# The first stage of a transformer layer rearranged: loads on two queues, weight folding ahead of the chunk loop, routing in four column tiles, one normalisation moved to POOL

## The chip, the cores and the metric

The kernel runs on one core of a Trainium2 chip. The time is the device time of one execution in microseconds (us), the median of three runs. The engines are TensorE (PE, whose weight loads are shown as PEld), VectorE (DVE), ScalarE (ACT), GpSimd (POOL) and SyncE (SP). Each executes its own queue in order, and they meet only at semaphores. DMAs are issued by SP, ACT and POOL and run on 16 shared DMA engines.

## The reference, cut to what matters

Input is a float32 tensor of 32 sequences, 256 tokens, 128 features, 8,192 tokens in all.

```python
xn = layernorm(x)                       # no gain, no bias
attn(xn):                               # low-rank attention + MLP block
    x1 = layernorm(xn, ln1_g, ln1_b)    # xn normalised a second time
    Q = einsum('bsd,dhr,hre->bhse', x1, q_U, q_V) + q_b     # K and V alike; 16 heads of 8
    h = xn + softmax(mask(Q K^T / sqrt(8))) V @ out_U @ out_V + out_b
    return h + gelu(layernorm(h, ln2_g, ln2_b) @ fc1_U @ fc1_V + fc1_b) @ fc2_U @ fc2_V + fc2_b
ffn(xn):                                # 9 experts, top 2 of each token
    probs = softmax(xn @ Wr)            # Wr is 128 x 9
    w, idx = top_k(probs, 2); w = w / sum(w)
    return sum over the two of w * (silu(xn @ Wg[e]) * (xn @ Wu[e])) @ Wd[e]
out = x + attn(xn) + ffn(xn)
```

## The kernel before, in words

Tokens are handled as 64 tiles of 128, in 16 chunks of 4 tiles. Four stages run one after another, each a block that all engines leave together: `prepare`, `attention`, `experts`, `mlp_and_combine`. Only `prepare` (L155 to L623) is changed. It has five kinds of work.

**Loads.** SP issues four loads of `x` (L240). ACT issues everything else: three `U` matrices, six pieces of the `V` matrices, 24 small loads (L309 to L325), the router weights (L326), and the expert weights in five DMAs (L327 to L330). Only then does ACT compute.

**Statistics.** DVE takes the statistics of all 64 tiles (L498) and turns them into mean and reciprocal deviations for the first and the second normalisation (L510 to L525).

**Fold.** The low-rank pairs are multiplied out once. PE waits for all small loads (L401) and turns `U` (L407 to L413), ACT copies the result out (L335 to L340), PE multiplies (L421), ACT copies again (L346 to L348). The products for the output projection and the MLP (L463 to L467), the scaling of the folded weights by ACT (L391 to L396) and the seven bias products on PE (L485 to L489) come after the chunk loop, some of them after routing.

**Chunk loop.** For each chunk DVE normalises four tiles into `xn` (L533), ACT scales them by the second reciprocal deviation into `xnr` (L357), PE transposes `xnr` (`turn`, L433), ACT copies the bank to `xt` (L364), and PE multiplies each transposed tile, as weights, with the 9 router columns (`score`, L441). DVE copies the 36 logits and multiplies the factor back (L540). SP stores `xn` and `xt` to DRAM in the order xt(c), xn(c+2) (L244, L248). Tiles `xn`, `xnr` and `xt` have two buffers each. The order of the queues is written out: PE does turn(c+2), score(c+1); ACT does scale, copy; DVE does normalise(c+3), copy_logits(c).

**Routing.** DVE picks the top two experts of every token and computes the slots (L569 to L617), with PE counting in between (L472 to L481). Meanwhile POOL issues 17 DMAs that blank the 8.8 MB table `slot_x` (L290), which begin when all `xn` are normalised. SP leaves the block only when these, and all stores, have landed (L259 to L263).

## Time and profile before

| what | value |
|---|---|
| median of 3 runs (lowest, highest) | 1107.15 us (1103.68, 1111.54) |
| the profiled execution's own time | 1107.88 us |
| its span, first to last instruction | 1106.2 us |
| busy share of PE, DVE, ACT, POOL over the span | 91%, 65%, 51%, 35% |
| mean granted TensorE clock | 0.929 of full speed |
| first stage: `prepare` | 0 to 122.2 us |

The first stage is a ninth of the span. It is read by itself, since the busy shares over the whole span are those of attention and the experts. "Granted clock" 1.00 stands for 2.4 GHz and 0.50 for 1.2 GHz.

### The profile page before, as it was taken

The page shows a single profiled execution, that of the slowest core. Times are in us where ns is not written, and L with a number is a line of the kernel's source. Part 1 is how long each engine was busy: PE and PEld are TensorE (multiplying, and loading weights), DVE is VectorE, ACT ScalarE, POOL GpSimd, SP SyncE. Part 2 cuts the span into 40 slices and gives each one's busy share as a digit, 9 for nine tenths or more (in the row PEclk, how much of TensorE's full clock was granted, in tenths as well). Part 3 has the DMA queues.
Part 4 walks back from the last instruction along what each step waited for, and adds up shares of the span by engine and source line. Part 5 has one row for each costly group of instructions (what it writes and reads, how often), then busy time and mean ns, then how long its engine had stood idle before and what let it go on. Part 6 is the DMA issues. An engine that isn't in the chain of part 4 may idle for free. (4 is left out here: it accounts for less than half of the span.)

```text
span 1106.2 us, 25514 instructions
## 1 busy us (share of the span) xinstructions
PE 1001.9 (91%) x7780; PEld 797.5 (72%) x7812; DVE 716.7 (65%) x3239; ACT 565.2 (51%) x1285; POOL 388.9 (35%) x509
## 2 busy tenths in 40 slices
PE   0797478999999999999999997999999999949997
PEld 0696255666666666666666655999999999939996
DVE  5344566777777777777777773555555554547887
ACT  0372025565566556556656674555555555525442
POOL 1003532434443343444334330444444444420110
PEclk9655659999999999999999997999999999969999
DMA  8669542444444444444444301222222222155774
GB/s 223 192 228 360 135 79 69 116 107 104 105 109 112 108 116 107 104 104 108 111 110 107 93 29 46 62 61 66 68 62 68 65 62 59 54 167 166 233 235 125
DMA packets 146754, 128.17 MB, mean 116 GB/s; under 512 B 18560, under 2 KB 128512, under 8 KB 146624
## 3 DMA queue, kind: packets, MB, share of 16 engines
q1 hardware_dynamic: 117344, 72.45, 23.8%
q0 software_dynamic: 17808, 47.35, 15.9%
q10 hardware_dynamic: 11472, 6.75, 2.3%
q8 instruction: 68, 1.11, 0.4%
q14 instruction: 62, 0.51, 0.2%
HBM read 57.68 MB, written 43.13 MB: 91 GB/s over the span
## 5 line engine op out<-in xcount | busy, mean ns | idle before, releaser
L1201 DVE CUSTOM_DVE_ANT_0 att_masked_st<-att_m_ps,att_mask_st 128x128 bf16<-128x128 f32 (+1 forms) x1024 | 312.0, 353 | 108.7 <-PE att_m_ps L916 72.1
L1106 ACT ACTIVATE att_probs<-att_t_ps 128x512 f32<-128x512 f32 x384 | 229.4, 598 | 190.5 <-PE att_t_ps L940 140.8
L834 POOL DMA_INDIRECT slot_x<-att_xs,att_slot_now x128 | 128.6, 1004 | 265.6 <-PE att_t_ps L940 169.1
L1369 POOL DMA_INDIRECT y_scratch<-moe_y,moe_row_now x136 | 131.3, 966 | 154.1 <-issue 68.7
L1509 DVE TENSOR_TENSOR moe_hidden<-moe_gate,moe_up_ps 128x352 f32<-128x352 f32 x136 | 70.9, 521 | 114.5 <-issue 84.2
L1429 PE MATMUL moe_y_ps<-w_down,moe_hidden_t 128*128 (+1 forms) x816 | 114.0, 276 | 2.4 <-issue 1.8
L1469 ACT ACTIVATE moe_gate<-moe_gate_ps 128x352 f32<-128x352 f32 x136 | 63.1, 464 | 95.9 <-PE moe_up_ps L1412 95.9
L940 PE MATMUL att_t_ps<-att_mask_ts,att_ident_b 128*128 128x256 bf16 (+1 forms) x352 | 111.1, 316 | 0.0
L1429 PEld LDWEIGHTS moe_y_ps<-w_down,moe_hidden_t 128*128 128x128 f32 (+1 forms) x816 | 101.7, 191 | 3.9 <-issue 3.8
L1201 DVE DVE_READ_ACCUMULATOR2_ANT att_row_max<- 128x1 f32 x1024 | 84.9, 83 | 0.2
L939 PE MATMUL att_t_ps<-even_stack,att_k_stack 97*128 97x512 f32 x192 | 81.2, 423 | 4.2 <-DMA even_stack<-att_neg_max 4.1
L955 PE MATMUL att_pv_ps<-att_probs,att_v_ones 128*32 128x256 f32 x1024 | 81.8, 391 | 0.0
L939 PE MATMUL att_t_ps<-att_odd_stack,att_k_stack 97*128 97x512 f32 x192 | 80.5, 420 | 1.3 <-DMA att_odd_stack<-att_neg_max 0.9
L940 PEld LDWEIGHTS att_t_ps<-att_mask_ts,att_ident_b 128*128 128x128 bf16 x384 | 37.5, 98 | 61.1 <-issue 54.7
L916 PE MATMUL att_m_ps<-att_k_stack,even_stack 96*128 96x256 f32 x256 | 71.2, 364 | 10.8 <-DMA even_stack<-att_q_lo 8.7
L1662 PEld LDWEIGHTS mlp_o_ps<-w,mlp_mid 128*128 128x128 f32 x512 | 66.4, 191 | 5.2
L916 PE MATMUL att_m_ps<-att_k_stack,att_odd_stack 96*128 96x256 f32 x256 | 68.1, 348 | 0.2 <-DVE att_row_max L1201 0.2
L1421 PE MATMUL moe_hidden_ps<-ident,moe_hidden 128*128 128x128 f32 (+1 forms) x408 | 67.1, 273 | 0.1
L1662 PE MATMUL mlp_o_ps<-w,mlp_mid 128*128 128x128 f32 x512 | 66.9, 275 | 0.0
L1702 ACT ACTIVATE mlp_mid<-mlp_f_ps,mlp_bias 128x512 f32<-128x512 f32 x64 | 44.0, 687 | 44.5 <-PE mlp_f_ps L1654 43.1
L916 PEld LDWEIGHTS att_m_ps<-att_k_stack,even_stack 96*128 96x128 f32 x256 | 42.8, 205 | 32.8 <-issue 28.4
L829 POOL DMA_DIRECT2D att_k_stack<-att_k_hi x64 | 36.8, 575 | 57.1 <-PE att_t_ps L940 30.7
(247 smaller groups left out, 2134.3 us busy)
## 6 DMA issues: line engine op xcount, KB each, us to landing
slot_x<-prep_blank POOLq DMA_DIRECT2D x17, 516.0 KB, 12.8
moe_x<-slot_x SPq DMA_DIRECT2D x34, 258.0 KB
att_xs<-xn_scratch SPq DMA_DIRECT2D x32, 256.0 KB
att_k_stack<-att_k_hi POOLq DMA_DIRECT2D x64, 128.0 KB
mlp_rows<-y_scratch POOLq DMA_DIRECT2D x16, 512.0 KB, 5.0
xn_scratch<-prep_xn SPq DMA_DIRECT2D x16, 256.0 KB, 2.6
xt_scratch<-prep_xt SPq DMA_DIRECT2D x16, 256.0 KB, 2.1
att_xt<-xt_scratch SPq DMA_DIRECT2D x16, 256.0 KB, 2.9
```

What stands on the lines that cost most here:

```text
L834: pool.indirect_dma_start(env["slot_x"][:], bass.IndirectOffsetOnAxis(ap=slot_now[c.parity][:, col:col + 1], axis=0), xs[c.parity][:, t, k ...
L916: last = pe.matmul(ps[:, n * SEQ:(n + 1) * SEQ], q[0:ROWS, g, i, hi:hi + P], k[0:ROWS, g, lo:lo + SEQ], start=True, stop=True)
L939: pe.matmul(by_lane, keys, q[rows, g, lanes, queries], start=True, stop=False, skip_group_check=True)
L940: pe.matmul(by_lane[:, :, 0:P], ident_b[:], mask_ts[:, lanes, :], start=False, stop=True, skip_group_check=True).then_inc(scores_done, 1)
L955: last = pe.matmul(pv_ps[32 * i:32 * i + 32, g * SEQ:(g + 1) * SEQ], v_ones[c.parity][:, 2 * b, g * LANES + i, :], pt, start=(g % 2 == 0), ...
L1106: act.activation(probs[:, m % PT, :], t_ps[m % 2][:], ACT.Exp).then_inc(exp_done, 1)
L1201: last = dve.tensor_tensor_reduce(out=masked_st[m % 2][:, part], in0=m_ps[m % 2][:, part], in1=mask_st[:, SEQ - width:], scale=1.0, scalar ...
L1369: pool.indirect_dma_start(env["y_dram"][:], bass.IndirectOffsetOnAxis(ap=row_now[q.parity][:, t:t + 1], axis=0), y[c.parity][:], None).the ...
L1421: last = pe.transpose(hidden_ps[0:n, k * P:(k + 1) * P], hidden[c.parity][:, col:col + n], ident[:])
L1429: last = pe.matmul(y_ps[:, 0:P], hidden_t[c.parity][0:n, k * P:(k + 1) * P], down_cols[0:n, ds(e * (NCH * P) + k * P, P)], start=(k == 0), ...
L1509: dve.tensor_tensor(hidden[c.parity][:], gate[c.parity][:], up_ps[c.parity][:, 0:FF], ALU.mult).then_inc(hidden_done, 1)
L1662: last = pe.matmul(o_ps[c.parity][:, t * P:(t + 1) * P], mid[c.parity][:, k, t * P:(t + 1) * P], w2[:, k, :], start=(k == 0), stop=(k == H ...
```

## The change

ACT keeps nine loads (`U`, `V`, counted on a semaphore of their own) and the router load. The 24 small loads and then the expert weights go to SP, behind the loads of `x` and before the first store. PE's fold of q, k, v waits for the nine loads only; the rest of the fold, with the scaling and the bias products, is done in front of the chunk loop. POOL makes `xnr` straight from `x` with the product of both reciprocal deviations; ACT's `scale` is gone. `score` has the router weights (padded from 9 to 32 columns with zeros) as the stationary side and the transposed tile as the moving side, each of the four tiles on its own 32 columns of the array. Its result is turned by 90 degrees, so ACT copies it to `by_expert`, and PE transposes that back (`score_back`), from where DVE reads the logits. DVE's `normalise` no longer waits for `xnr`. Loops that indexed with `ds` are written out.

```diff
-w_router = s.sb("w_router", [P, EXPERTS])
+w_router = s.sb("w_router", [P, 32])
...
+both_rstd = s.sb("both_rstd", [P, tiles])
+by_expert = s.two("by_expert", [P, P])
...
+        small = [0]
+        def load(dst, src, columns=False):
+            sp.dma_start(dst, src, allow_slow_non_contiguous=columns).then_inc(small_loaded, 16)
+            small[0] += 16
+        load(out_u[:], w["out_U"])
+        load(out_v[:], w["out_V"])
+        load(fc1_u[:], w["fc1_U"])
+        load(fc1_v[:], w["fc1_V"])
+        load(fc2_u[:], w["fc2_U"].rearrange("(c p) r -> p c r", p=P))
+        load(fc2_v[:], w["fc2_V"])
+        for dst, name in ((ln1_g, "ln1_g"), (ln1_b, "ln1_b"), (ln2_g, "ln2_g"), (ln2_b, "ln2_b")):
+            load(dst[:], w[name].rearrange("(p o) -> p o", o=1), True)
+        load(v_b[:], w["v_b"].rearrange("h e -> (h e)").partition_broadcast(P))
+        load(out_bias[:], w["out_b"].partition_broadcast(P))
+        load(fc2_bias[:], w["fc2_b"].partition_broadcast(P))
+        load(fc1_b[:], w["fc1_b"].rearrange("(c p) -> p c", p=P), True)
+        for dst, name in ((q_b, "q_b"), (k_b, "k_b")):
+            by_lane = w[name].rearrange("(g i) (e o) -> i e g o", i=LANES, o=1)
+            for i in range(LANES):
+                load(dst[32 * i:32 * i + 32, :], by_lane[i], True)
+        assert small[0] == 16 * N_SMALL
+        sp.wait_ge(x_loaded[XL - 1], 16)
+        sp.dma_start(w_gate_up[:, :, 0:FF].bitcast(F32), w["Wg"].rearrange("e d i -> d e i")).then_inc(experts_loaded, 16)
+        sp.dma_start(w_gate_up[:, :, FF:2 * FF].bitcast(F32), w["Wu"].rearrange("e d i -> d e i")).then_inc(experts_loaded, 16)
+        for c, (at_row, rows) in enumerate(FF_CHUNKS):
+            sp.dma_start(w_down[0:rows, :, c, :], w["Wd"][:, at_row:at_row + rows, :].rearrange("e p d -> p e d")).then_inc(experts_loaded, 16)
         def store_xn(c):
+            sp.wait_ge(xn_ready, c + 1)
+            sp.dma_start(env["xn_tiles"][:, c * TPC:(c + 1) * TPC, :], xn[c % 2][:]).then_inc(xn_stored[c % 2], 16)
...
+        store_xn(0)
+        store_xn(1)
+        for c in range(chunks):
+            store_xt(c)
+            if c + 2 < chunks:
+                store_xn(c + 2)
...
+        pool.memset(w_router[:], 0.0).then_inc(router_cleared, 1)
...
+        pool.wait_ge(ln_ready, 1)
+        for c in range(chunks):
+            if c >= 2:
+                pool.wait_ge(xt_turned, c - 1)
+            for t in range(TPC):
+                tile = c * TPC + t
+                last = pool.tensor_scalar(xnr[c % 2][:, t, :], x_all[:, tile, :], mean[:, tile:tile + 1], both_rstd[:, tile:tile + 1],
+                                          ALU.subtract, ALU.mult)
+            last.then_inc(xnr_ready, 1)
         pool.wait_ge(xn_ready, chunks)
...
+            act.dma_start(u_in[k][:], w[f"{n}_U"].rearrange("d h r -> d (h r)")).then_inc(qkv_loaded, 16)
...
+        act.wait_ge(router_cleared, 1)
+        act.dma_start(w_router[:, 0:EXPERTS], w["Wr"]).then_inc(router_loaded, 16)
...
         act.wait_ge(fold_pe, 7)
         for k in range(2):
             act.copy(raw_qkv[:, k, :].rearrange("p (i e g) -> p g i e", i=LANES, e=DH),
                      bank[6][:, k * P:(k + 1) * P].rearrange("p (g i e) -> p g i e", i=LANES, e=DH)).then_inc(fold_act, 1)
         act.copy(raw_qkv[:, 2, :], bank[6][:, 2 * P:3 * P]).then_inc(fold_act, 1)
+        act.wait_ge(fold_pe, 8)
+        act.copy(ut_small[0:RANK_OUT, 0:P], bank[7][0:RANK_OUT, 0:P]).then_inc(fold_act, 1)
+        act.copy(ut_small[0:RANK_MLP, P:2 * P], bank[7][0:RANK_MLP, P:2 * P]).then_inc(fold_act, 1)
+        act.wait_ge(fold_pe, 9)
+        act.copy(ut_fc2[:], bank[0][0:RANK_MLP, :]).then_inc(fold_act, 1)
+        act.wait_ge(small_loaded, 16 * N_SMALL)
         act.mul(g_q[:], ln1_g[:], float(DH) ** -0.5).then_inc(fold_act, 1)
...
+        def copy_xt(c):
+            act.wait_ge(xt_turned, c + 1)
+            if c >= 2:
+                act.wait_ge(xt_stored[c % 2], 16 * (c // 2))
+            act.copy(xt[c % 2][:], bank[c % 2][:]).then_inc(xt_ready, 1)
+        def copy_by_expert(c):
+            act.wait_ge(routed_t, c + 1)
+            if c >= 2:
+                act.wait_ge(logits_ready, c - 1)
+            act.copy(by_expert[c % 2][:], bank[2 + c % 2][:, 0:P]).then_inc(by_expert_ready, 1)
+        copy_xt(0)
+        for c in range(chunks):
+            if c + 1 < chunks:
+                copy_xt(c + 1)
+            copy_by_expert(c)
+        act.wait_ge(gap_ready, 1)
+        act.activation(gap_exp[:], gap[:], ACT.Exp).then_inc(gap_exped, 1)
...
     @block.tensor
     def _(pe):
         pe.wait_ge(const_ready, N_CONST)
+        pe.wait_ge(qkv_loaded, 16 * N_QKV)
         for r in range(6):
             for j in range(4):
                 pair = 4 * (r % 2) + j
                 last = pe.transpose(bank[r][0:PR, j * P:(j + 1) * P], u_in[r // 2][:, pair * PR:(pair + 1) * PR], ident[:])
             last.then_inc(fold_pe, 1)
...
+        pe.wait_ge(small_loaded, 16 * N_SMALL)
+        pe.transpose(bank[7][0:RANK_OUT, 0:P], out_u[:], ident[:])
+        pe.transpose(bank[7][0:RANK_MLP, P:2 * P], fc1_u[:], ident[:]).then_inc(fold_pe, 1)
+        for c in range(HCH):
+            last = pe.transpose(bank[0][0:RANK_MLP, c * P:(c + 1) * P], fc2_u[:, c, :], ident[:])
+        last.then_inc(fold_pe, 1)
+        pe.wait_ge(fold_act, 12)
+        pe.matmul(bank[1][:, 0:P], ut_small[0:RANK_OUT, 0:P], out_v[:], start=True, stop=True)
+        pe.matmul(bank[2][:], ut_small[0:RANK_MLP, P:2 * P], fc1_v[:], start=True, stop=True)
         for c in range(HCH):
             last = pe.matmul(bank[3][:, c * P:(c + 1) * P], ut_fc2[:, c * P:(c + 1) * P], fc2_v[:], start=True, stop=True)
         last.then_inc(fold_pe, 1)
+        pe.wait_ge(fold_act, 21)
+        pe.matmul(bank[6][:, 0:1], raw_qkv[:, 0, :], ln1_b[:], start=True, stop=True)
+        pe.matmul(bank[6][:, 1:2], raw_qkv[:, 1, :], ln1_b[:], start=True, stop=True)
+        for c in range(HCH):
+            pe.matmul(bank[6][:, 2 + c:3 + c], raw_w1[:, c * P:(c + 1) * P], ln2_b[:], start=True, stop=True)
+        pe.matmul(bank[6][:, P:2 * P], b_rows[:], raw_qkv[:, 2, :], start=True, stop=True).then_inc(fold_pe, 1)
+        def turn(c):
+            pe.wait_ge(xnr_ready, c + 1)
+            if c >= 2:
+                pe.wait_ge(xt_ready, c - 1)
+            for t in range(TPC):
+                last = pe.transpose(bank[c % 2][:, t * P:(t + 1) * P], xnr[c % 2][:, t, :], ident[:])
+            last.then_inc(xt_turned, 1)
+        def score(c):
+            pe.wait_ge(xt_ready, c + 1)
+            if c >= 2:
+                pe.wait_ge(by_expert_ready, c - 1)
+            for t in range(TPC):
+                last = pe.matmul(bank[2 + c % 2][32 * t:32 * t + 32, 0:P], w_router[:], xt[c % 2][:, t * P:(t + 1) * P], start=True, stop=True,
+                                 skip_group_check=True)
+            last.then_inc(routed_t, 1)
+        def score_back(c):
+            pe.wait_ge(by_expert_ready, c + 1)
+            if c >= 2:
+                pe.wait_ge(logits_copied, c - 1)
+            pe.transpose(bank[4 + c % 2][:, 0:P], by_expert[c % 2][:], ident[:]).then_inc(logits_ready, 1)
+        pe.wait_ge(router_loaded, 16)
+        turn(0)
+        turn(1)
+        score(0)
+        for c in range(chunks):
+            if c + 2 < chunks:
+                turn(c + 2)
+            if c + 1 < chunks:
+                score(c + 1)
+            score_back(c)
         pe.wait_ge(gap_ready, 1)
+        pe.wait_ge(logits_copied, chunks)
...
+        step(dve.tensor_tensor(both_rstd[:], rstd[:], rstd2[:], ALU.mult))
+        dve.sem_inc(ln_ready, 1)
         step(dve.tensor_tensor(std2[:], var[:], rstd2[:], ALU.mult))
...
+        def normalise(c):
+            if c >= 2:
+                dve.wait_ge(xn_stored[c % 2], 16 * (c // 2))
...
+        def copy_logits(c):
+            dve.wait_ge(logits_ready, c + 1)
+            dve.tensor_tensor(logits[:, c * TPC:(c + 1) * TPC, :], bank[4 + c % 2][:, 0:P].rearrange("p (t e) -> p t e", e=32)[:, :, 0:EXPERTS],
+                              std2[:, c * TPC:(c + 1) * TPC].unsqueeze(2).to_broadcast([P, TPC, EXPERTS]), ALU.mult).then_inc(logits_copied, 1)
+        normalise(0)
+        normalise(1)
+        normalise(2)
+        for c in range(chunks):
+            if c + 3 < chunks:
+                normalise(c + 3)
+            copy_logits(c)
...
-        dve.wait_ge(fold_pe, 13)
+        dve.wait_ge(fold_pe, 11)
...
```

## Rows read from the trace of the kernel before

**Rows 1.** Busy time by windows: PE, PEld, DVE, ACT, POOL, clock, DMA share, GB/s.
```profile
70.00:80.00 10.00, 10.00 (x50) 10.00 (x51) 5.06 (x22) 7.23 (x21) 0.00 (x0) 0.50 0.65 215
300.00:310.00 10.00, 9.93 (x91) 6.22 (x92) 7.85 (x46) 6.55 (x12) 1.94 (x2) 1.00 0.45 136
```

**Rows 2.** Timeline of the loads (start, duration, both in us); last line: landing of `v_v`.
```profile
8.53 2.73 ACTq L298 DMA_DIRECT2D prep_ln_g<-in_L_attn_ln_g  x1
10.84 2.92 SPq L240 DMA_DIRECT2D prep_x_all<-in_L_attn_hidden_states  x1
24.34 0.53 ACTq L298 DMA_DIRECT2D prep_fc_v<-in_L_attn_fc_V  x1
26.75 10.77 ACTq L330 DMA_DIRECT2D w_down<-in_L_ffn_Wd  x3
...
DMA to landing us min/median/max: 7.0/7.3/7.6
```

**Rows 3.** Timeline of the fold before the chunk loop.
```profile
27.70 1.92 PE L407 MATMUL prep_bank<-ident,prep_u_q 128*96 128x128 f32 x8 [27.70 <-DMA prep_fc_v<-in_L_attn_fc_V]
32.30 0.23 DVE L525 TENSOR_TENSOR prep_std<-prep_var,prep_rstd 128x64 f32<-128x64 f32 x1
40.12 3.54 PEld L421 LDWEIGHTS prep_bank<-prep_v_q,prep_ut 96*128 96x128 f32 x16
50.69 0.61 ACT L346 COPY prep_raw_qkv<-prep_bank 128x128 f32<-128x128 f32 x2 [8.05 <-PE prep_bank L421]
52.81 2.19 PE L433 MATMUL prep_bank<-ident,prep_xnr 128*128 128x128 f32 x8 [2.21 <-ACT prep_xnr L357]
```

**Rows 4.** Timeline of one period of the chunk loop.
```profile
80.92 0.90 PEld L433 LDWEIGHTS prep_bank<-ident,prep_xnr 128*128 128x128 f32 x4
81.81 1.83 PEld L441 LDWEIGHTS prep_bank<-prep_w_router,prep_xt 128*128 128x128 f32 x8
82.26 0.59 ACT L364 COPY prep_xt<-prep_bank 128x512 f32<-128x512 f32 x1 [0.69 <-PE prep_bank L433]
83.37 0.90 PEld L433 LDWEIGHTS prep_bank<-ident,prep_xnr 128*128 128x128 f32 x4
```

**Rows 5.** Timeline of a store of `xn` and the normalisation that waits for it.
```profile
60.15 0.36 SPq L244 DMA_DIRECT2D xn_scratch<-prep_xn  x1
62.45 1.12 DVE L533 TENSOR_SCALAR prep_xn<-prep_x_all,prep_mean,prep_rstd 128x128 f32<-128x128 f32 x4 [0.80 <-DMA xn_scratch<-prep_xn]
```

**Rows 6.** Timeline after the loop: rest of the fold, end of routing.
```profile
93.15 0.50 PEld L463 LDWEIGHTS prep_bank<-prep_out_v,prep_ut_small 96*128 96x128 f32 x2 [0.45 <-issue]
97.69 0.59 ACT L385 COPY w<-prep_bank 128x512 f32<-128x512 f32 x1 [1.12 <-PE prep_bank L467]
102.98 0.39 ACT L391 ACTIVATE wq<-prep_raw_qkv,prep_g_q 128x128 f32<-128x128 f32 x1
111.22 0.59 PE L485 MATMUL prep_bank<-prep_ln_b,prep_raw_qkv 128*128 128x1 f32 x2
113.81 0.78 PE L489 MATMUL prep_bank<-prep_raw_qkv,prep_b_rows 128*128 128x128 f32 x2
122.23 3.51 POOL L811 MEMSET even_stack<- 128x4096 f32 x1 [27.48 <-POOLq L234]
```

**Rows 7.** Timeline in attention: matmuls of 32 columns, and the next 128-column one.
```profile
305.91 0.64 PE L961 MATMUL att_pv_ps<-att_probs,att_v_ones 128*32 128x128 f32 x16
306.49 0.51 PE L916 MATMUL att_m_ps<-att_k_stack,att_odd_stack 96*128 96x256 f32 x2
```

**Rows 8.** Groups by line, POOL's operations: busy us, mean ns, idle before.
```profile
L850 POOL TENSOR_TENSOR att_xn<-att_xn,out_bias 128x512 f32<-128x512 f32 x16 | 20.7, 1291 | 0.3
L274 POOL TENSOR_SCALAR_AFFINE_SELECT ident<-ident 128x128 f32<-128x128 f32 x1 | 0.3, 290 | 0.2 <-POOL prep_ones L271 0.2
```

**Rows 9.** The blanking of `slot_x`: POOL's issues, then the window in which DMA falls silent.
```profile
85.62 8.08 POOL L290 DMA_DIRECT2D slot_x<-prep_blank  x15 [80.99 <-DVE prep_xn L533]
112.00:116.00 4.00, 2.58 (x12) 2.28 (x11) 3.63 (x15) 0.00 (x0) 0.00 (x0) 0.50 0.07 28
```

More of the change, by code:

```diff
@@ L388, in _ @@
-                act.activation(gap_exp[:], gap[:], ACT.Exp).then_inc(gap_exped, 1)
                 act.wait_ge(fold_act, 16)
@@ L423, in _ @@
                 last.then_inc(fold_pe, 1)
-                pe.wait_ge(fold_act, 9)
-                pe.wait_ge(router_loaded, 16)
-                def turn(c, first):
-                    pe.wait_ge(xnr_ready, c.index + 1)
-                    if not first:
-                        pe.wait_ge(xt_ready, c.index - 1)
-                    for t in range(TPC):
-                        last = pe.transpose(bank[c.parity][:, t * P:(t + 1) * P], xnr[c.parity][:, t, :], ident[:])
-                    last.then_inc(xt_turned, 1)
@@ L436, in score @@
-                def score(c, of_four, first):
-                    pe.wait_ge(xt_ready, c.index + 1)
-                    if not first:
-                        pe.wait_ge(logits_copied, c.index - 3)
-                    for t in range(TPC):
-                        last = pe.matmul(bank[2 + of_four][:, t * EXPERTS:(t + 1) * EXPERTS], xt[c.parity][:, t * P:(t + 1) * P],
-                                         w_router[:], start=True, stop=True)
-                    last.then_inc(logits_ready, 1)
@@ L465, in _ @@
-                pe.wait_ge(fold_act, 9)
+                pe.wait_ge(small_loaded, 16 * N_SMALL)
[5 more added lines that the diff above has]
+                pe.wait_ge(fold_act, 12)
```

154 lines of the change are left out of this document (15 added, 139 removed).

## The prediction, made before the changed kernel was run

> **What bounds the kernel now.** The change touches the first stage alone, so I read the chain of waits only to see that everything runs in sequence behind that stage (the chain that ended last begins in the MLP stage and says nothing of `prepare`), and then windows and timeline of `prepare` by itself. Attention's first instruction comes at 122.2 us [rows 6], so a microsecond taken from the stage is one from the total as long as nothing else holds the stage's end. The stage has three stretches.
>
> First, up to 52.8 us: PE starts its first transpose at 27.70 us, released by the last small load, and the chunk loop's first transpose at 52.81 us [rows 3]. DVE was through with the statistics at 32.5 us [rows 3]; the fold is what is late. It is late because ACT issues loads until 26.75 + 10.77 = 37.5 us [rows 2] before it copies anything, and because 48 small matmuls take from 40.12 to 50.69 us [rows 3].
>
> Second, the chunk loop from 52.8 to 93.15 us, 40.3 us [rows 3, 6]. One period is 83.37 - 80.92 = 2.45 us, and PE fills it: 0.89 us of transposes, then 1.56 us of routing matmuls [rows 4]. In that stretch PE is 10.00 us busy in 10, ACT 7.23, DVE 5.06, DMA 0.65, at a granted clock of 0.50 [rows 1], that is 1.2 GHz.
>
> Third, routing from 93.15 to 122.2 us, 29.1 us [rows 6], mostly a DVE chain with PE counting in between.
>
> **The change part by part.** *Loads and first half of the fold.* ACT now issues only nine loads before the router's. The last of the nine is out before 8.53 us, where ACT now goes on to the small loads, and lands at most 7.6 us later [rows 2]: 16.1 us instead of 27.7 for PE's start. The 24 transposes cost 0.222 us each at the loop's pace (0.89 / 4 [rows 4]), 5.3 us, to 21.4 us; ACT, idle by then, copies beside them. The 48 matmuls cost the same 10.6 us [rows 3], to 32.0 us. I cost them at the slow level of the clock, since nothing denser than before runs there.
>
> *Small loads on SP.* SP is through with issuing `x` at 10.84 + 2.92 = 13.8 us; the 24 small loads took ACT from 8.53 to 24.87 us, 16.3 us, and the last landed 27.70 - 24.34 = 3.4 us after issue [rows 2, 3]. So they are in at 13.8 + 16.3 + 3.4 = 33.5 us at the latest; about 31 us if the 2.73 us of the first [rows 2] is a full queue that SP does not meet. The fold goes on at about 33.0 us (ends 32.0 and 33.5).
>
> *Second half of the fold, now ahead of the loop.* Six transposes at 0.222 and a copy, 2.0 us, to 35.0; products and their copies as at 93.15 to 97.69 + 0.59, 5.1 us, to 40.1; five scalings at 0.39, 1.9 us, to 42.0; bias products 111.22 to 113.81 + 0.78, 3.4 us [rows 6], to 45.4 us. Where they come from they were hidden: the products under DVE's routing, the bias products under the same chain, so their removal there gains nothing. Here they are on the path, 12.4 us of it, and are the price of starting the loop with PE and ACT clear. The loop starts at 45.4 us instead of 52.8: **7.4 us gained** (bounds of the start 43 and 49).
>
> *Expert weights on SP.* They follow the small loads, from 30.1 us, for 10.8 us for three [rows 2] and about 1.2 for two short ones: SP reaches its first store at 42 us, which lands some 3 us later. Behind that store stand DVE's third normalisation and, behind that, the first copy of logits, which is due at 45.4 + 3.5. Cost nothing; a further 4 us in that queue would show one for one.
>
> *POOL's normalisation.* No POOL operation of this kind is in the trace. From below: one pass over 128x128 takes 0.29 us; a two-input pass over 128x512 takes 1.29, a quarter of it 0.32 [rows 8]. From above: subtract and multiply as two passes, 0.58. I take 0.35, near the quarter since it has the same width and one read less, against two scalars per partition to fetch: 1.4 us for a chunk (1.2 to 2.3). The first two chunks are ready before 37 us, since its inputs are there at 32.5. The extra DVE multiplication costs 0.23 us [rows 3], off the path.
>
> *Column tiles.* Attention's 16 matmuls of 32 columns with 128 moving columns take 0.64 us, and the next full-width one starts 0.58 us after the first of them [rows 7], at a granted clock of 1.00 [rows 1]. At half of that, the eight of a chunk take 0.6 us instead of 1.56. The upper end is no overlap at all, 1.6. The new transpose back is 0.22, its copy on ACT at most 0.59 where 1.27 of scaling disappear [rows 4]. PE: 0.89 + 0.6 + 0.22 = 1.7 us for a chunk.
>
> The trace shows full-width and 32-column matmuls following each other without a visible gap [rows 7]. The Trainium skill (TensorEngine Tiling (Array Packing), Tiling Modes) says that changing the tiling mode drains the engine, and the loop changes it twice per chunk; by that PE's 1.7 us would be longer by two drains, still below what comes next.
>
> *What bounds the loop next.* DVE may write a buffer of `xn` only when its store has landed: 1.12 us of normalising, 2.30 us from issue to the normalisation that waited for it [rows 5], and 0.1 to 0.9 us until SP comes to it behind a store of `xt`. That makes 3.5 to 4.3 us for two chunks, 1.8 to 2.15 for one. I take a period of 2.1 us. Around 14 full periods stand about 5.0 us: two turns, a copy and the first scores 2.4, and at the end a score, a copy, a transpose back and a copy of logits 2.6. The loop takes 5.0 + 14 x 2.1 = 34.4 us against 40.3: **5.9 us gained**.
>
> *End of the stage.* Routing is unchanged, 29.1 us. The stage ends at 45.4 + 34.4 + 29.1 = 108.9 us. The blanking DMAs begin 7.5 us ahead of the loop's end and were silent by about 112 us [rows 9], some 27 us after their start: 72.3 + 27 = 99 us, still covered by routing. If the loop's last part were much faster they would come next, with 10 us to spare.
>
> Sum: 7.4 + 5.9 = 13.3 us. The profiled execution took 1107.9 us, so 1094.6; it lies 0.7 us above the median of the runs shown. I forecast **1094.5 us**.
>
> **The rivals.** *(A) DVE and POOL exclude each other.* The trace cannot tell: POOL does no arithmetic in the loop today. If every normalising instruction of either engine held the other up, a chunk would cost 1.12 + 1.4 = 2.5 us, and the stage's gain would be 7.4 + 40.3 - 5.0 - 35.0 = 7.7 us: 1100 us. Against it: DVE's time for four is partly start-up of each instruction, in which POOL could get through. By this kernel's rows the engines are 1.1 and 1.4 us busy, so even in turns they barely exceed the old period. The Trainium skill (SBUF — State Buffer, Who interferes with whom) states such an exclusive port pair for DVE's `tensor_scalar` in a two-port mode against any GpSimd operation; no row here bears it out or refutes it.
>
> *(B) POOL is slow, and the kernel slower than before.* The place is POOL's four instructions per chunk. At 0.58 us each and in turns with DVE the period is 4 x 0.58 + 1.12 = 3.4 us, the loop 52.6 us, the total 1107.9 - 7.4 + 12.3 = 1112.8 us. It decides from a period of (40.3 + 7.4 - 5.0) / 14 = 3.05 us, which is 0.48 us per POOL instruction in turns with DVE, or 0.76 alone.
>
> *(C) Column tiles do not overlap here*, with four tiles of different data: PE 0.89 + 1.6 + 0.22 and the switches, 2.8 us; gain 3.5 us, 1104.4 us. Against it stands attention's row.
>
> *(D) The loop starts late.* Small loads behind `x` in SP's queue, or the stores behind 4.5 MB of expert weights, cost 5 us more: 1099.5 us.
>
> *(E) PE is granted the full clock* somewhere in the fold, now that it runs in one piece. It halves at most the 27 us of fold: up to 10 us more, some 1088 us. Against it: PE was just as busy between 40 and 50.7 us and in the loop, and stayed at 0.50 [rows 1].
>
> **How the numbers follow.** Forecast 0.47, A 0.21, B 0.09, C 0.07, D 0.09, E 0.07. The forecast's own range, start 43 to 48 and period 1.8 to 2.3, is 1088 to 1100. A measurement can tell about 1% (11 us) from no change; that needs a period below 2.3 at the forecast's start. Faster by more: 0.9 of the forecast, E, and a third of A and D, 0.59. Slower by more than 1%: B beyond 3.8 us per period or several delays at once, 0.05. Within: 0.36. The range runs from 1087 (E, and the fast end of the forecast) to 1106 (A, C, D with the scatter of the runs); B and the far end of E are left out.
>
> **What would show it.** Right: PE's first transpose near 16 us; q, k, v products done near 32; the first `xnr` transposes at 45 us and 2.1 us apart; DVE idle before `xn` on the store; router matmuls of a chunk in about 0.6 us; POOL 0.35 us each; POOL's blanking from 72 us; attention from 109 us. Wrong: POOL's instructions above 0.48 us, or PE waiting for `xnr` each chunk (A, B); router matmuls 0.2 us apart (C); a wait of DVE or PE for loads beyond 46 us (D). The forecast would also fail if attention, started 13 us earlier, gave part of it back in its own first chunks.

## The result, and the profile after: 1112.05 us instead of 1094.5

Over 20 runs each the changed kernel took 1112.05 us (1109.84 to 1114.47), the kernel before 1107.58 us (1102.48 to 1111.54): a ratio of 1.0037, interval 1.0026 to 1.0048. That is within 1%, on the slow side, and 17.5 us above the forecast. A second series of the same kernel gave 1110.78 against 1107.50 us, 1.0038 (1.0024 to 1.0053). The profiled execution took 1112.97 us, of which the span is 1111.2.

I read the changed kernel in the same order as the old one. First the timeline of PE from the first transpose to the chunk loop (start and duration in us; what stands in brackets is idle time and who ended it):

```profile
13.87 1.92 PE L404 MATMUL prep_bank<-ident,prep_u_q 128*96 128x128 f32 x8 [13.87 <-DMA prep_v_v<-in_L_attn_v_V]
17.80 1.86 PE L411 MATMUL prep_bank<-prep_v_q,prep_ut 96*128 96x16 f32 x16
21.30 1.94 PE L411 MATMUL prep_bank<-prep_v_v,prep_ut 96*128 96x16 f32 x16
30.05 0.45 PE L416 MATMUL prep_bank<-ident,prep_out_u 128*96 128x128 f32 x1 [6.81 <-DMA prep_k_b<-in_L_attn_k_b]
43.15 1.92 PE L440 MATMUL prep_bank<-ident,prep_xnr 128*128 128x128 f32 x8
```

The fold starts at 13.87 us instead of 27.70 [rows 3], runs to 23.24 us, then PE stands for 6.81 us until the last small load is in, and the loop's first transpose comes at 43.15 us. Before, it came at 52.81 us [rows 3]: 9.7 us gained, 2.3 more than forecast. Now windows of that stretch, of the loop and of the same 10 us as in [rows 1] (PE, PEld, DVE, ACT, POOL busy; clock; DMA share; GB/s):

```profile
16.00:24.00 8.00, 7.23 (x63) 7.11 (x61) 7.76 (x39) 3.16 (x8) 0.00 (x0) 0.96 0.49 141
24.00:31.00 7.00, 0.95 (x5) 0.81 (x6) 6.04 (x29) 0.26 (x2) 0.00 (x0) 0.50 0.28 43
70.00:80.00 10.00, 6.37 (x40) 3.35 (x40) 4.11 (x17) 2.56 (x6) 10.00 (x14) 0.50 0.50 171
```

Two things are new. First, PE ran at the full clock in the middle of the fold: the 48 products take 5.4 us (17.80 to 23.24), where they took 10.6 us [rows 3]. The clock column alone does not show this. It reads 1.00 in the kernel before too, from 28 to 36 us, while eight transposes took 1.92 us there [rows 3], and it reads 1.00 here at 13.87 us, where eight take the same 1.92 us as at 43.15 us and a reading of 0.50. The durations are to be read beside it. Second, in the loop PE fell from 10.00 busy in 10 to 6.37, while POOL went from 0.00 to 10.00: the bound has moved to POOL. One period of the loop shows how, against [rows 4]:

```profile
69.34 8.15 POOL L326 TENSOR_SCALAR prep_xnr<-prep_x_all,prep_mean,prep_both_rstd 128x128 f32<-128x128 f32 x10
73.49 1.11 PE L440 MATMUL prep_bank<-ident,prep_xnr 128*128 128x128 f32 x4 [1.12 <-POOL prep_xnr L326]
74.54 0.66 PE L449 MATMUL prep_bank<-prep_xt,prep_w_router 128*32 128x128 f32 x8
74.64 0.59 ACT L379 COPY prep_xt<-prep_bank 128x512 f32<-128x512 f32 x1 [2.35 <-PE prep_bank L440]
75.12 0.48 PE L457 MATMUL prep_bank<-ident,prep_by_expert 128*128 128x128 f32 x1
75.64 0.20 DVE L535 TENSOR_TENSOR prep_logits<-prep_bank,prep_std 128x36 f32<-128x36 f32 x1 [1.96 <-PE prep_bank L457]
75.75 1.16 DVE L528 TENSOR_SCALAR prep_xn<-prep_x_all,prep_mean,prep_rstd 128x128 f32<-128x128 f32 x4
76.72 0.69 PE L440 MATMUL prep_bank<-ident,prep_xnr 128*128 128x128 f32 x2 [1.12 <-POOL prep_xnr L326]
```

The transposes of two chunks begin 76.72 - 73.49 = 3.23 us apart, where it was 2.45. Everyone else waits: PE for POOL, ACT for PE, DVE for PE. POOL alone has no gap between its instructions. The groups by line give its price (count, busy us, mean ns, idle before):

```profile
L326 POOL TENSOR_SCALAR prep_xnr<-prep_x_all,prep_mean,prep_both_rstd 128x128 f32<-128x128 f32 x64 | 51.6, 818 | 33.2 <-DVEq L520 26.7 <-PE prep_bank L440 6.5
```

The waits of the loop, 43 to 97 us, say who stood for whom (total, times, longest, in us). PE stood 16.5 us for POOL:

```profile
PE prep_bank L440 <- POOL prep_xnr L326: 16.5, 14, 1.8
DVE prep_xn L528 <- DMA xn_scratch<-prep_xn: 15.8, 3, 14.3
ACT prep_xt L379 <- DMA xt_scratch<-prep_xt: 6.3, 2, 3.7
```

POOL itself stood once, for 6.5 us up to 44.2 us: it had filled both buffers of `xnr`, and PE had not begun to empty them. At 0.81 us from start to start (3.23 / 4) its 64 instructions from 31.41 us on would have ended near 83 us without that wait, by estimate, instead of at 89.48.

Last, the timeline at the loop's end and at the stage's end, against [rows 6]:

```profile
89.48 9.19 POOL L332 DMA_DIRECT2D slot_x<-prep_blank  x17
...
93.18 0.20 DVE L535 TENSOR_TENSOR prep_logits<-prep_bank,prep_std 128x36 f32<-128x36 f32 x1 [0.26 <-PE prep_bank L457]
...
122.58 3.51 POOL L802 MEMSET even_stack<- 128x4096 f32 x1 [23.91 <-POOLq L237]
```

The account of the stage: the loop starts 9.7 us earlier, it lasts 93.38 - 43.15 = 50.2 us instead of 40.3, 9.9 us more, and routing takes 29.2 us as before. The stage ends at 122.58 us, where it ended at 122.23. The whole rearrangement is paid back inside the loop.

### The profile page after: what moved, and what is told of

Same layout as the page of the kernel before. It is cut to its first block and busy times, and to the rows that moved or that the text cites. A ratio compares the mean times of both kernels' runs of the same rounds, so it can differ in the third digit from the quotient of the medians.

```text
span 1111.2 us, 25566 instructions
## 1 busy us (share of the span) xinstructions
PE 990.7 (89%) x7796; PEld 770.2 (69%) x7828; DVE 717.9 (65%) x3240; ACT 551.3 (50%) x1237; POOL 440.3 (40%) x574
## 3 DMA queue, kind: packets, MB, share of 16 engines
q8 instruction: 69, 1.13, 0.4%
HBM read 57.68 MB, written 43.13 MB: 91 GB/s over the span
## 5 line engine op out<-in xcount | busy, mean ns | idle before, releaser
L326 POOL TENSOR_SCALAR prep_xnr<-prep_x_all,prep_mean,prep_both_rstd 128x128 f32<-128x128 f32 x64 | 51.6, 818 | 33.2 <-DVEq L520 26.7
## 6 DMA issues: line engine op xcount, KB each, us to landing
slot_x<-prep_blank POOLq DMA_DIRECT2D x17, 516.0 KB, 11.1
```

## The experiments

The theory to be tested: POOL's instruction with two values per partition costs 0.80 us and alone sets the period; the loads, the fold and the column tiles are worth about what was forecast. Rivals: DVE and POOL hold each other up at a shared port; column tiles save nothing; the stores hold the loop; the rearranged stage slows the later stages. "Before" always means the kernel before, run on the same chip beside the experiment; different experiments ran on different chips, so their ratios compare better than their times. The edits are given in short. The end of the stage is read from the same instruction as above, the first one of attention on POOL.

**One edit to the changed kernel: ACT makes `xnr` again.**

```diff
-pool: xnr[c % 2][:, t, :] = (x_all[:, tile, :] - mean) * both_rstd
+act.activation(xnr[c % 2][:, t, :], xn[c % 2][:, t, :], ACT.Identity, scale=rstd2[:, ...])   # after xn_ready, ahead of copy_xt
+dve: normalise(c) waits for xnr_ready again
```

> The changed kernel, but the twice normalised x is made by ACT from xn, as in the kernel before (DVE waits for it again). Theory P (POOL's instructions of 0.8 us are the loop's period and nothing else is): period 2.1 to 2.3 us instead of 3.23, the loop 34 to 37 us instead of 50, the first stage ends near 108 us instead of 122.6. Theory S (the period is held by the stores or by the new chain of copies on ACT as well): period 2.8 us or more, stage end 116 us or later. Theory R for the total (the rest of the kernel, from the stage's end on, is 988.7 us after and 984.0 us before, and the rearranged stage itself costs the rest 4 to 5 us): total = stage end + 989, so 1097 us under P. If the 4.7 us belong to when attention starts or to chance of one profile: stage end + 984, so 1092 us.

Measured: 1101.16 us, ratio 0.9942 (0.9921 to 0.9962); stage end 112.61 us. Taking POOL out of the loop gives back 10 us of the stage. From the third chunk (50.18 us) to the last (80.06 us) PE's transposes are 2.30 us apart in the mean, the upper end of theory P; the stage still ends 4.6 us later than theory P had it. The timeline (SP's issues, DVE, PE) shows what is late next:

```profile
40.86 2.48 SPq L278 DMA_DIRECT2D xn_scratch<-prep_xn  x2
42.42 1.91 PE L443 MATMUL prep_bank<-ident,prep_xnr 128*128 128x128 f32 x8
47.70 2.13 DVE L532 TENSOR_SCALAR prep_xn<-prep_x_all,prep_mean,prep_rstd 128x128 f32<-128x128 f32 x8 [14.48 <-DMA xn_scratch<-prep_xn]
50.18 1.12 PE L443 MATMUL prep_bank<-ident,prep_xnr 128*128 128x128 f32 x4 [5.26 <-ACT prep_xnr L383]
```

The first store of `xn` is issued at 40.86 us, behind the expert weights in SP's queue, and lands near 47.7. DVE has waited 14.48 us for it, ACT scales what DVE made, and PE stops for 5.26 us at the third chunk. This is rival D of the prediction, a late start of the stores. In the changed kernel it is hidden, since POOL makes `xnr` from `x` and is slower anyway.

**One edit to the kernel before: POOL makes `xnr`.**

```diff
-scale(c) on ACT, and DVE's wait for xnr_ready
+POOL's loop over tensor_scalar(xnr, x_all, mean, both_rstd, subtract, mult), as in the changed kernel
```

> The kernel before with only this part of the change: POOL makes xnr, ACT's scale is gone. Loads, fold and router matmuls as before. Theory P: period 3.2 us instead of 2.45, loop longer by about 14 x 0.8 = 11 us, the total 1118 us. Theory X (POOL is slow only beside DVE, or only in the new kernel): period below 2.7 us, total within 4 us of before. The loop starts as before near 52 us.

Measured: 1117.44 us, ratio 1.0087 (1.0060 to 1.0114); stage end 130.64 us, 8.4 us later than before. PE's weight loads show the period, against [rows 4]; the group shows POOL's price in this kernel:

```profile
61.70 0.72 PEld L431 LDWEIGHTS prep_bank<-ident,prep_xnr 128*128 128x128 f32 x4 [0.78 <-POOL prep_xnr L294]
64.90 0.72 PEld L431 LDWEIGHTS prep_bank<-ident,prep_xnr 128*128 128x128 f32 x4 [0.68 <-POOL prep_xnr L294]
```

```profile
L294 POOL TENSOR_SCALAR prep_xnr<-prep_x_all,prep_mean,prep_both_rstd 128x128 f32<-128x128 f32 x64 | 51.1, 813 | 41.1 <-DVEq L524 26.7 <-PE prep_bank L431 14.4
```

The period is 3.2 us (64.90 - 61.70), though loads, fold and router matmuls are as before. This one part of the change costs 8.4 us of the stage and 10.7 us of the median.

**Loads and fold alone**: the changed kernel with ACT's scaling and the old routing.

```diff
+scale(c) on ACT; score(c) with xt as weights and 9 moving columns
-POOL's xnr, w_router of 32 columns, by_expert, score_back
```

> The changed kernel's loads and fold ahead of the loop, with the loop of before (ACT makes xnr, router matmuls 128x128 by 9 columns, no transpose back). If loads and fold are a gain of their own: the loop starts at 43 to 44 us instead of 52.8, its period is 2.45 us as before, the stage ends near 113 us, total 1098 us (or 1103 if the rest loses 5 us). If moving the fold ahead costs what it saves: stage end 120 us or more.

Measured: 1103.70 us, ratio 0.9966 (0.9946 to 0.9986); loop start 42.41, period 2.45 us, stage end 115.81 us.

```profile
69.60 0.90 PEld L441 LDWEIGHTS prep_bank<-ident,prep_xnr 128*128 128x128 f32 x4
72.06 0.90 PEld L441 LDWEIGHTS prep_bank<-ident,prep_xnr 128*128 128x128 f32 x4
```

The loop starts 10.4 us earlier but the stage ends only 6.4 us earlier; the stop on the first store takes the rest. Beside the first experiment, which differs by the column tiles and the transpose back alone, they are worth 115.81 - 112.61 = 3.2 us of the stage.

**POOL's forms measured by themselves**, in its idle time at the start of the changed kernel, on tiles that nothing else uses:

```diff
+for _ in range(2): pool.tensor_copy(out(), trial_in[:, 0:P])
+for _ in range(2): pool.tensor_scalar(out(), trial_in[:, 0:P], 2.0, None, ALU.mult)
+for _ in range(2): pool.tensor_scalar(out(), trial_in[:, 0:P], 1.0, 2.0, ALU.subtract, ALU.mult)
+for _ in range(2): pool.tensor_scalar(out(), trial_in[:, 0:P], at_one[:, 0:1], None, ALU.mult)
+for _ in range(2): pool.tensor_scalar(out(), trial_in[:, 0:P], at_one[:, 0:1], at_one[:, 1:2], ALU.subtract, ALU.mult)
+pool.tensor_scalar(out(4), trial_in[:], at_one[:, 0:1], at_one[:, 1:2], ALU.subtract, ALU.mult)
+for _ in range(2): pool.tensor_tensor(out(), trial_in[:, 0:P], ones[:], ALU.mult)
```

> The changed kernel with 13 more POOL instructions on scratch tiles in POOL's idle time between 5 and 31 us; nothing reads them. 128x128 float32: copy, one operation with a constant, two operations with constants, one operation with a per-partition scalar, two operations with two per-partition scalars, a two-input multiply; and 128x512 with two per-partition scalars. Theory A (the per-partition scalars cost, each a fixed amount): copy and constants near 0.3 us, one scalar 0.5 to 0.55, two scalars 0.8, and 128x512 with two scalars 0.8 + 0.4 to 0.8. Theory B (two operations cost per element): two constants 0.5 to 0.8 us as well, and 128x512 about 2.5 us or more. Theory C (the sharing of ports with DVE costs): two scalars well below 0.8 us here, where DVE takes statistics or idles.

Measured, in the order of the diff (start, duration of the group; x2 is two instructions):

```profile
5.26 0.52 POOL L330 COPY prep_trial<-prep_trial_in 128x128 f32<-128x128 f32 x2
5.77 1.06 POOL L332 TENSOR_SCALAR prep_trial<-prep_trial_in 128x128 f32<-128x128 f32 x2
6.81 1.26 POOL L334 TENSOR_SCALAR prep_trial<-prep_trial_in 128x128 f32<-128x128 f32 x2
8.07 1.18 POOL L336 TENSOR_SCALAR prep_trial<-prep_trial_in,prep_at_one 128x128 f32<-128x128 f32 x2
9.24 1.56 POOL L338 TENSOR_SCALAR prep_trial<-prep_trial_in,prep_at_one 128x128 f32<-128x128 f32 x2
10.80 2.06 POOL L340 TENSOR_SCALAR prep_trial<-prep_trial_in,prep_at_one 128x512 f32<-128x512 f32 x1
12.84 0.44 POOL L342 TENSOR_TENSOR prep_trial<-prep_trial_in,prep_ones 128x128 f32<-128x128 f32 x1
```

A copy costs 0.29 us, as the select of [rows 8] did. One operation with a constant costs about 0.53, with a value per partition 0.59; two operations 0.64 with constants and 0.78 with values per partition. A two-input pass of the same size costs 0.44. So the price hangs on the form, and the two rows that I had taken as nearest are of the cheap forms. Neither theory fits whole: A had the constants near 0.3 us, B had the wide tile at 2.5 us or more, and it took 2.06. The 0.78 is there with POOL by itself, so DVE beside it can account for at most the 0.02 to 0.04 us by which the loop's instruction is longer. This is one execution of one kernel.

**Expert weights issued by POOL instead of SP**, on the first experiment's kernel.

```diff
-sp.dma_start(w_gate_up ..., w_down ...)      # five, ahead of the first store
+pool.dma_start(w_gate_up ..., w_down ...)    # after x_loaded
```

> The kernel of e1 (ACT makes xnr), with the five expert-weight DMAs issued by POOL, which has nothing to do there, and not by SP in front of the first stores. Theory Q (the queue: in e1 the first store of xn goes out at 40.9 us because SP issues weights until then; DVE waits 14.5 us for it and PE 5.3 us behind that): first store near 33 us, no wait of PE at the third chunk, stage end 5 us earlier than e1's 112.6, total 4 to 5 us below e1. Rival (the DMA engines are full with the weights whichever queue issues them, so the store lands as late): the third chunk's wait stays above 3 us, total within 1.5 us of e1.

Measured: 1107.49 us, ratio 1.0012 (0.9998 to 1.0027); stage end 121.12 us. SP's queue was free, and the stage ended 8.5 us later than with the weights on it. PE's timeline, and the DMA share of two windows (second-last number):

```profile
42.61 0.45 PE L419 MATMUL prep_bank<-ident,prep_out_u 128*96 128x128 f32 x1 [16.81 <-DMA prep_k_b<-in_L_attn_k_b]
```

```profile
20.00:30.00 10.00, 5.80 (x37) 5.69 (x36) 8.94 (x42) 0.72 (x3) 4.18 (x5) 0.60 0.87 260
30.00:40.00 10.00, 0.00 (x0) 0.00 (x0) 3.48 (x14) 0.00 (x0) 0.00 (x0) 0.50 1.03 263
```

The weights' transfers fill the 16 engines from 20 us on, and the small loads, issued at the same time, land 12.6 us later than in the changed kernel (42.6 against 30.05 us). The loop starts at 55.71 us instead of 42.42, and with so late a start the third chunk waits only 0.41 us. Neither expectation was met. The queue was part of what makes the first store late: it is issued at 32.80 us instead of 40.86. But the DMA engines are full, and a store takes up to 9.9 us to land where the longest took 6.8. The Trainium skill (DMA: Bandwidth & Descriptors, Issuing engines are not separate DMA queues) says that DMAs of all issuing engines interleave on the same 16 engines; the trace agrees, with the 12.6 us.

**The same, with a wait for the needed loads only.** PE and ACT wait for the first ten small loads (the weights and gains that the fold uses); the other fourteen have a semaphore of their own.

```diff
-pe.wait_ge(small_loaded, 16 * N_SMALL)     # ACT alike
+pe.wait_ge(fold_loaded, 16 * N_FOLD)       # the first ten; dve waits for the rest before q_bias
```

> The kernel of e5, and PE's second half of the fold waits for the first ten small loads only (matrices and layer norm gains), not for all 24; the others are waited for by DVE at the end. In the changed kernel PE stands still from 23.2 to 30.05 us for the last of them. If that wait is the start's limit: the loop starts 5 to 7 us earlier than in e5 (near 37 us), but not before the statistics allow, total 4 to 6 us below e5, near 1091 us. If DVE's statistics and first normalisation (33 us) and the stores set the pace instead: less than 2 us below e5.

Measured: 1095.12 us, ratio 0.9911 (0.9886 to 0.9936); loop start 39.03, stage end 109.86 us. PE's wait is gone: the turn of `out_U` starts at 25.95 us. The loop starts 16.7 us and the stage ends 11.3 us earlier than in the kernel above; I had expected 5 to 7 us. The third chunk still stops (PE, DVE, PE):

```profile
25.95 0.43 PE L422 MATMUL prep_bank<-ident,prep_out_u 128*96 128x128 f32 x1
44.12 2.14 DVE L535 TENSOR_SCALAR prep_xn<-prep_x_all,prep_mean,prep_rstd 128x128 f32<-128x128 f32 x8 [10.16 <-DMA xn_scratch<-prep_xn]
46.60 1.11 PE L446 MATMUL prep_bank<-ident,prep_xnr 128*128 128x128 f32 x4 [5.07 <-ACT prep_xnr L386]
```

The first store of `xn` goes out at 32.97 us, 7.9 us earlier than behind the weights in SP's queue (40.86), and has landed at 44.12, only 3.6 us earlier (47.70): it is 11.1 us on its way instead of 6.8.

**The same, with ACT making `xnr` straight from `x`**, so that it hangs on no store.

```diff
-act.wait_ge(xn_ready, c + 1)
-act.activation(xnr, xn,    Identity, scale=rstd2)
+act.activation(xnr, x_all, Identity, scale=both_rstd, bias=both_shift)   # both_shift = -mean * both_rstd
```

> The kernel with split small loads (its PE and ScalarE wait only for the first ten small loads, ScalarE scales xn), with one edit: ScalarE makes xnr straight from x, with scale = product of the reciprocal deviations and bias = -mean times it, so PE's transposes no longer hang on DVE's xn and its stores. Theory S (the stop of 5.07 us at the third chunk is the store of xn landing late and holding DVE, then ScalarE): the stop vanishes, the period becomes that of ScalarE, 1.27 + 0.59 + 0.27 = 2.1 us, the stage ends near 104 us instead of 109.9, total about 1090 against 1095.1. Rival T (the store of xt waits in the same queue behind the store of the third xn, so ScalarE's copy of the fourth chunk stops instead): PE stops at the third or fourth chunk for about 5 us as before, stage end 108 to 110, total 1094 to 1095.

Measured: 1091.53 us, ratio 0.9852 (0.9829 to 0.9874); stage end 105.17 us. The stop has shrunk from 5.07 to 0.78 us, and ACT sets the period (2.18 us), as PE's and ACT's timelines show:

```profile
43.13 1.12 PE L448 MATMUL prep_bank<-ident,prep_xnr 128*128 128x128 f32 x4 [0.78 <-ACT prep_xnr L387]
...
66.70 1.66 ACT L387 ACTIVATE prep_xnr<-prep_x_all,prep_both_shift,prep_both_rstd 128x128 f32<-128x128 f32 x4
68.25 0.58 ACT L373 COPY prep_xt<-prep_bank 128x512 f32<-128x512 f32 x1
68.72 0.27 ACT L379 COPY prep_by_expert<-prep_bank 128x128 f32<-128x128 f32 x1
68.88 1.67 ACT L387 ACTIVATE prep_xnr<-prep_x_all,prep_both_shift,prep_both_rstd 128x128 f32<-128x128 f32 x4
```

The theory of the store holds, its rival (the store of `xt` in the same queue stops the fourth chunk instead) does not. This is the fastest kernel of the study.

**Column tiles undone in that kernel.**

```diff
-score(c) in four column tiles, copy_by_expert(c), score_back(c)
+pe.matmul(bank[2 + c % 4][:, t * EXPERTS:(t + 1) * EXPERTS], xt[..t..], w_router[:])
```

> The same kernel as the one in which ScalarE makes xnr straight from x, with one part of the change undone: routing has the transposed tiles as weights and nine moving columns again, four weight loads a chunk, and there is no transpose back and no copy of by_expert. Theory O (column tiles overlap, 0.58 to 0.66 us for a chunk against 1.56): PE is 0.89 + 1.56 = 2.45 us a chunk and sets the period at 2.45 instead of ScalarE's 2.1; with the shorter end of the loop the kernel is 3 to 5 us slower than the one with column tiles. Rival C (the column tiles save nothing once the transpose back and its copy are counted): the same time or faster.

Measured: 1094.92 us, ratio 0.9896 (0.9874 to 0.9917); stage end 107.86 us, PE's period 2.46 us:

```profile
54.48 1.09 PE L441 MATMUL prep_bank<-ident,prep_xnr 128*128 128x128 f32 x4
56.94 1.09 PE L441 MATMUL prep_bank<-ident,prep_xnr 128*128 128x128 f32 x4
```

The column tiles are worth 2.7 us of the stage and 3.4 us of the median here, with 3.2 us in the pair above. Rival C is refuted.

**Only POOL's price changed**, in the changed kernel: a plain copy, and one operation with one value per partition. The first leaves out the normalisation in `xnr`, the second the mean, so neither kernel computes the layer; all other instructions are the changed kernel's.

```diff
-pool.tensor_scalar(xnr, x_all, mean, both_rstd, ALU.subtract, ALU.mult)
+pool.tensor_copy(xnr, x_all)                              # first kernel
+pool.tensor_scalar(xnr, x_all, both_rstd, None, ALU.mult) # second kernel
```

> The changed kernel with one edit: POOL copies x into xnr (a plain copy of 128x128, 0.29 us in the run of POOL's forms) instead of subtracting and multiplying by two values per partition; xnr is then x without its normalisation. Theory P (the price of POOL's instruction, 0.80 us, is the failed step, the others held but for the late first store): period about 2.2 us, a stop of some 5 us of the third chunk on the first store of xn, stage end 112 to 113, total 1100 to 1102. Rival F (the forecast's other steps hold in full, no stop): stage end 108, total 1096 to 1097. Rival X (the loop is held by something else than POOL, as the store of xn or PE): period above 2.6, total above 1104.

> The changed kernel with one edit: POOL multiplies x by one value per partition (0.594 us in the run of POOL's forms, near the upper bound of 0.58 of the forecast) and does not subtract the mean; xnr is then x without its mean taken off. Theory P: four instructions set the period, 4 x 0.594 + 0.03 = 2.41 us, with the stop on the first store partly hidden: stage end 113 to 116, total 1102 to 1105, so that the forecast's upper bound would still have been faster than before. Rival X: the period stays above 2.8 us and the total above 1107.

Measured: with the copy 1096.84 us, ratio 0.9920 (0.9890 to 0.9950), stage end 107.59 us; with one operation 1098.61 us, 0.9940 (0.9918 to 0.9961), stage end 109.73 us. The groups of POOL in the two kernels, and PE's transposes of the second:

```profile
L326 POOL COPY prep_xnr<-prep_x_all 128x128 f32<-128x128 f32 x64 | 16.3, 299 | 51.3 <-DVEq L519 27.0 <-PE prep_bank L439 24.2
```

```profile
L326 POOL TENSOR_SCALAR prep_xnr<-prep_x_all,prep_both_rstd 128x128 f32<-128x128 f32 x64 | 37.5, 604 | 34.5 <-DVEq L519 26.4 <-PE prep_bank L439 8.1
```

```profile
72.11 1.12 PE L439 MATMUL prep_bank<-ident,prep_xnr 128*128 128x128 f32 x4 [0.20 <-POOL prep_xnr L326]
74.42 1.11 PE L439 MATMUL prep_bank<-ident,prep_xnr 128*128 128x128 f32 x4 [0.20 <-POOL prep_xnr L326]
```

From 0.80 us to 0.60 and 0.30 the stage ends 12.9 and 15.0 us earlier, and no other line was touched. (The granted clock moved with it: 0.63 and 0.75 from 60 to 80 us, against 0.50 in the changed kernel.) At 0.60 the period is 2.31 us and POOL still sets it. At 0.30 POOL waits for PE, and the loop takes 35.2 us (43.16 to 78.38), where the forecast had 34.4. Its period is 2.17 us in the mean, where the forecast had 2.1, and now the stores weigh as the forecast said: ACT waits 20.3 us (14 times) for stores of `xt`, DVE 22.8 us (12 times) for stores of `xn`. I had expected a stop of 5 us on the first store in these two; the longest stop of PE was 2.9 us in the first, and both came in 3 to 6 us below my figures, in the first near those of rival F.

**The later stages.** The changed kernel and the kernel before were run again as they are, twice, the second time the changed one in five rounds.

> The kernel before once more, for a second profile of it. The rest of the kernel, from the stage's end to the end of the span, took 984.0 us in its profile and 985.5 to 989.2 us in the profiles of five kernels whose stages after the first are the same code. If that is chance of one profile (theory N), this one gives 985 to 989, and its first stage may end away from 122.2 us with the clock's phase, by up to 5 us. If the rearranged first stage makes the rest slower (theory R), it gives 983 to 985 again, with the stage's end at 122.

> The changed kernel once more, for a second profile of it. Under theory N the rest of the kernel takes 985 to 989 us and need not repeat its 988.7; under theory R it takes 988 to 990 again. The first stage ends within 1 us of 122.6, since POOL sets its loop and POOL's time does not hang on TensorE's clock.

> The changed kernel as it is, against the kernel before, to see whether what its medians have beyond the first stage (about 4 us, where the ends of the first stage differ by 0.5 us) is there again. Theory R (the changed stage makes the later stages slower by 3 to 4 us): ratio 1.003 to 1.005 again. Rival N (chance of that set of runs): ratio 0.999 to 1.002.

> The kernel before as it is, for one more profile of the stages behind the first: between the end of the first stage and the end, 984 us as in its two other profiles (theory R) or anywhere between 982 and 989 us as in the other kernels (rival N).

Measured, from the end of the first stage to the end of the span: before 984.0, 983.8 and 989.7 us; changed 988.6, 984.1 and 986.6 us. The profiles overlap, and the one of `before_b` lies above all of the changed kernel. But the ratio of the five rounds was 1.0038 again, so the difference of the medians, 3.3 to 4.5 us, is not chance. The three profiles of each kernel show less of it: their spans are 1.4 us apart in the mean (1107.5 and 1108.9). Of this 0.75 us are there at the end of the first stage (121.68 and 122.43) and all 1.4 us at the first product with V in attention (162.9 and 164.3). The other 2 to 3 us of the medians are in no profile.

The other runs have the same gap. If the median is compared with that of the kernel before beside it, and the movement of the stage's end (from 121.68) is taken off, 2.5 to 5.0 us are left in the six series of kernels in which SP issues the expert weights, and 0.5 to 2.0 us in the five others. With POOL's copies the stage ends 14.1 us earlier and the median falls by 9.1 us only. Each figure rests on one profile for the stage's end, and no run was made for the split, so it is a hint; where the time goes is left open.

## Why the prediction was wrong, point by point

- *POOL's normalisation*: this is the step that failed. I priced the instruction at 0.35 us with an upper bound of 0.58; it measured 0.78 alone and 0.80 to 0.82 in the loop. The lower value was a quarter of a two-input pass over 128x512, 0.32; the same pass over 128x128 takes 0.44. The bound was two plain passes of 0.29 each; yet a pass that takes even one value per partition costs 0.59. The bound was no bound, because it was built from rows of another form of instruction.
- *What bounds the loop next*: I said the store of `xn`, at 2.1 us. It was POOL, at 3.23 us. Over 14 periods that is 14 x 1.13 = 15.8 us, and it explains the miss of the stage: 108.9 + 15.8 - 2.3 (earlier start) = 122.4 us, against 122.58 measured. With POOL's price put near the forecast's, the mean period falls to 2.17 and 2.34 us, the stage ends at 107.6 and 109.7 us (forecast 108.9) and the total is 1096.8 and 1098.6 us. For the stage the other steps of the forecast held together, with errors that cancel in part: a start 2.3 us early against a loop 0.8 us long.
- *A microsecond of the stage is one of the total*: this I took without a price, and it held only in part. With POOL's copies the stage ended 1.3 us before the forecast and the total lay 2.3 us above it; the 2.5 to 5.0 us that such kernels lose against their stage are not explained.
- *Rival B* is what happened, by its second reading: it put the point of decision at 0.76 us per instruction with POOL alone. With the start as measured the point is (40.3 + 9.7 - 5.0) / 14 = 3.21 us for a chunk, 0.80 for an instruction, and there the stage came out level; the rest of the slowdown is not in the stage. That its figure of 1112.8 us lies near the 1112.05 measured is luck: it stands for 0.58 us in turns with DVE and a later start. I gave it 0.09, and left it out of the range.
- *Rival A*, DVE and POOL excluding each other: refuted in this kernel. In full turns a chunk would take 4 x 0.78 + 1.12 = 4.24 us; it took 3.23. POOL's instruction takes 0.80 to 0.82 us in the loop and 0.78 alone; DVE's four take 1.16 us against 1.12 [rows 5]. The Trainium skill (SBUF — State Buffer, Who interferes with whom) says that the shared port pair is an exclusive lock, which DVE's `tensor_scalar` takes when it runs in a two-port mode. The trace shows 0.01 to 0.04 us per instruction; in which mode DVE ran, no run shows.
- *Loads and first half of the fold*: PE started at 13.87 us (forecast 16.1) and was through at 23.24 (forecast 32.0), since it was granted the full clock; *rival E* came true in part. It bought nothing, because the small loads landed at 30 us (forecast 31 to 33.5) and PE stood for them. In the two other profiles of the same kernel the clock fell back sooner, PE was through at 25.97 and 26.28 us, and the loop began at 42.83 and 43.13 us all the same. A forecast with the clock at half speed hid that wait.
- *Second half of the fold*: forecast 12.4 us from the last small load to the loop; measured 43.15 - 30.05 = 13.1. The start was forecast at 45.4, and came at 43.15.
- *Expert weights on SP*: I costed them at nothing, with "a further 4 us would show one for one". In the changed kernel they cost nothing, as POOL hides them; without POOL they cost a stop of about 5 us. The place was right, and the term that was too small is the way of the first store: 6.8 us to land where I had put 3. Taking the weights out of SP's queue brings its issue 7.9 us forward and its landing 3.6 us, since the DMA engines stay full. (The weights are 4,752 KB by their issues; I had written 4.5 MB.)
- *Column tiles*: 0.6 us for a chunk forecast, 0.58 to 0.66 measured, at half clock. Their worth, 2.7 to 3.2 us, only shows when POOL is out of the way. Where PE fills its time, as in the kernel with POOL's copies from 54 to 58 us (window and two transposes below), a chunk costs it 1.85 us, 0.14 more than the forecast's 0.89 + 0.6 + 0.22. Whether that is the price of switching between tiling modes, which the prediction named, the trace does not separate.

```profile
54.00:58.00 4.00, 4.00 (x28) 2.58 (x29) 2.92 (x13) 1.69 (x5) 1.96 (x8) 0.50 0.89 297
54.19 1.06 PE L439 MATMUL prep_bank<-ident,prep_xnr 128*128 128x128 f32 x4
56.04 1.06 PE L439 MATMUL prep_bank<-ident,prep_xnr 128*128 128x128 f32 x4
```

- *End of the stage*: routing 29.2 us as forecast, and the blanking stays hidden though it began only at 89.48 us.

## What to carry to other kernels

Moving work to an idle engine is priced by that engine's row for that very form of instruction: number of operations, and whether its operands are constants, values per partition or tiles. Where no such row exists, the bound from above must not be built from the cheapest form, nor from a share of a wider tile: two passes of the two-input form at its 128x128 price, 0.88 us, would have been a bound here, two copies were not. The break-even price is to be compared with that bound before anything else. When a bound moves, look for the waits that the new bound hides (here the first store, the wait for all small loads); removing them took the ratio from 0.9942 to 0.9852 (1101.16 to 1091.53 us).

## What the runs showed of the hardware that I had not expected

POOL's time per 128x128 float32 instruction runs from 0.29 us (copy) over 0.44 (two tiles), 0.53 (one constant), 0.59 (one value per partition) and 0.64 (two constants) to 0.78 us (two values per partition); the last takes 2.06 us on 128x512, so by estimate from these two sizes some 0.35 us of it do not depend on size.

PE's busy time alone does not tell which clock TensorE is granted. The kernel before had PE 10.00 busy in 10 at 0.50 [rows 1]. The kernel with POOL's copies had PE 4.00 busy in 4 at 0.50 from 54 to 58 us, read 1.00 from 60 us on, and fell back to 0.50 near 67 us, when PE had been busy for 1.3 of 4 us (PE, PEld, DVE, ACT, POOL busy, then the clock):

```profile
60.00:70.00 10.00, 6.22 (x65) 3.62 (x64) 5.68 (x23) 3.49 (x10) 4.62 (x20) 0.83 0.74 248
```

From 40 to 80 us all profiles of kernels that route with the transposed tile as weights read 0.50: three of the kernel before and three of experiments. The six experiments on the changed kernel's loop that keep the column tiles and make `xnr` faster than 0.78 us per tile read 0.50 to 0.75 in the two halves of that stretch, each above 0.50 in at least one. Why is not shown.
